# Splitting V's low product into its own matmul, a fourth side bank, and a new order of the query and key transposes in a causal attention kernel

## The reference, cut to what matters

```python
y = x * rsqrt(mean(x * x) + RMS_EPS) * rms_w
y = einsum('bsm,cm->bsc', y, w_in)             # q: 32 heads, k and v: 8 heads, each 64 wide
q, k = rope(q), rope(k)
qk = einsum('bghsd,bgxpd->bghsp', q, k) * 64 ** -0.5
attn = softmax(where(causal, qk, -inf))
o = einsum('bghsp,bgxpd->bghsd', attn, v)      # 4 query heads of a group share k and v
y = einsum('bsc,mc->bsm', o, w_out)            # then x + y, and the feed-forward layer
```

## Time and profile before

| | value |
|---|---|
| median of three runs | 2312.43 us |
| the profiled execution | 2314.37 us, its span 2312.5 us |
| busy share PE, DVE, POOL, ACT | 89%, 68%, 59%, 44% |
| matmuls and weight loads | 17919 and 17919 |
| mean granted TensorE clock | 0.965 of 2.4 GHz |

### The profile page before, as it was taken

The page is one execution under the profiler, slowest core; times in us unless marked ns, Lnnn a source line. Parts: engine busy times, 40 slices in busy tenths (PEclk is TensorE's granted clock), DMA queues, the critical chain, the costliest instruction groups (busy, mean ns, idle before and its releaser), DMA issues. The chain is left out here.

```text
span 2312.5 us, 53405 instructions
## 1 busy us (share of the span) xinstructions
PE 2048.1 (89%) x17919; PEld 1242.3 (54%) x17919; DVE 1572.3 (68%) x2975; ACT 1020.7 (44%) x2216; POOL 1363.8 (59%) x1468
## 2 busy tenths in 40 slices
PE   2489988997998898899889889988989888999998
PEld 1255655565565556556556655655655444444443
DVE  8368867966986796688679668868966666222211
ACT  3245545554555555456555545555554331211210
POOL 5357777785777778577777757777770333212311
PEclk7789999999999999999999999999999999999999
DMA  5421121122112212211221221122116451000000
GB/s 167 133 42 34 34 51 47 31 50 48 34 34 52 49 30 49 48 34 34 52 53 30 46 47 34 34 52 56 31 39 212 159 163 41 1 18 14 5 18 19
DMA packets 228784, 122.74 MB, mean 53 GB/s; under 512 B 187168, under 2 KB 208416, under 8 KB 226976
## 3 DMA queue, kind: packets, MB, share of 16 engines
q1 hardware_dynamic: 228512, 119.26, 20.5%
HBM read 50.53 MB, written 25.17 MB: 33 GB/s over the span
## 5 line engine op out<-in xcount | busy, mean ns | idle before, releaser
L776 POOL TENSOR_TENSOR pl<-p 128x512 f16<-128x512 f32 (+3 forms) x801 | 766.2, 970 | 271.1 <-ACT p L621 269.7
L706 DVE TENSOR_REDUCE mpart<-a_ps 128x1 f32<-128x512 f32 (+3 forms) x1288 | 734.3, 599 | 244.1 <-PE a_ps L538 164.1
L621 ACT ACTIVATE p<-a_ps 128x512 f32<-128x512 f32 (+3 forms) x1283 | 663.9, 532 | 457.0 <-PE a_ps L553 255.3
L568 PE MATMUL a_ps<-v,p 128*128 128x129 f16 x4352 | 555.6, 222 | 28.8 <-DVE pl L698 15.6
L535 PE MATMUL a_ps<-k_hl,q_hh 128*128 128x512 f16 (+3 forms) x1288 | 448.6, 354 | 86.9 <-DVE v L728 51.5
L570 PE MATMUL a_ps<-v,pl 128*128 128x65 f16 x4352 | 519.2, 194 | 0.0
L552 PE MATMUL a_ps<-q_hh,k_hl 128*128 128x512 f16 (+3 forms) x1283 | 453.0, 353 | 55.7 <-DMA q_lm<-qk_lo 55.7
L568 PEld LDWEIGHTS a_ps<-v,p 128*128 128x128 bf16 x4352 | 405.5, 98 | 149.5 <-DVE pl L698 38.8
L553 PE MATMUL a_ps<-q_lm,k_h 128*128 128x512 f16 (+3 forms) x1283 | 451.4, 352 | 0.0
L570 PEld LDWEIGHTS a_ps<-v,pl 128*128 128x128 f16 x4352 | 396.1, 99 | 94.5 <-issue 5.0
L698 DVE TENSOR_TENSOR pl<-p 128x512 f16<-128x512 f32 (+2 forms) x482 | 421.8, 878 | 13.3 <-ACT p L621 13.3
(11 more groups left out here) (99 smaller groups left out, 2762.5 us busy)
## 6 DMA issues: line engine op xcount, KB each, us to landing
attn_scratch<-onorm SPq DMA_DIRECT2D x32, 512.0 KB, 3.0
p_att<-attn_scratch SPq DMA_DIRECT2D x64, 256.0 KB, 3.4
raw<-ffn_t SPq DMA_DIRECT2D x12, 1024.0 KB, 6.9
wraw<-w_in_t SPq DMA_DIRECT2D x9, 768.0 KB, 5.2
resid_scratch<-xin SPq DMA_DIRECT2D x4, 1024.0 KB, 4.3
raw<-w_out_t SPq DMA_DIRECT2D x1, 4096.0 KB, 15.2
x<-resid_scratch SPq DMA_DIRECT2D x4, 1024.0 KB, 6.8
out<-x SPq DMA_DIRECT2D x16, 256.0 KB, 2.0
```

What stands on the lines that cost most here:

```text
L568: nc.tensor.matmul(o, p_high[:, i % RING, t * P:(t + 1) * P], v[:, par, j, 0:VU], start=(j == 0 and t % 2 == 0), stop=False, skip_group_ch ...
L621: nc.scalar.activation(p32[:, i % RING, r * P:CHUNK], sbank(i)[:, r * P:CHUNK], ACT.Exp, scale=SCALE).then_inc(exp_done, 1)
L706: nc.vector.reduce_max(mpart[:, u % 2, t, kk:kk + 1], side_bank(part, ("piece", ahead, u, i))[:, 0:width], AX.X)\
L776: nc.gpsimd.tensor_tensor(pl[:, i % RING, cols], p32[:, i % RING, cols], p_high[:, i % RING, cols], ALU.subtract).then_inc(low_pool, 1)
```

## The change

A value row of V becomes [V high, 1, spare, V low]: the low part starts at column 66 (`VL`). P high now meets [V high, 1] in a matmul of 65 columns, P high again meets V low in one of 64 that adds into the same 64 output columns, and P low meets [V high, 1] as before. Each query tile's output is 65 wide, four fit one bank (260 numbers), and the bank that is freed goes to the side work, which now has four (`SIDE`). ScalarE copies 260 instead of 516 numbers per partition, and GpSimd's `osum` goes. In units where a step has sometimes two pieces they come earlier by up to a slot (`i * n // m == j`), and where a piece comes every few steps it comes at the start of that stretch.

In `TRANSFERS`, `hh` gets a due step six steps ahead of the unit two before its own, `k` moves from 1.5 to 4 steps behind the last low part, and `lm` is due 2.5 slots after the unit's last piece. The opening issues keys after the first `hh`, and the low parts of units 0 and 1 ahead of later ones.

```diff
-VW = DH + 1 + DH + 1
-VU = 2 * DH + 1
+VU = DH + 1
+VL = VU + 1
+VW = VL + DH
...
+SIDE = 4
...
-            pieces = [(ahead, w, i) for i in range(j * m // n, (j + 1) * m // n)]
+            pieces = [(ahead, w, i) for i in range(m) if i * n // m == j]
...
-    timed = [(FIRST_STEP[2] + 2, ("store", 3, -1))]
-    timed += [(FIRST_STEP[HG * (c + 1)] + OUT_LAG + 4, ("store", c, 0)) for c in range(NCH - 1)]
+    timed = [(FIRST_STEP[4] - 2, ("store", 3, -1))]
+    timed += [(FIRST_STEP[HG * (c + 1) + 1] + 4, ("store", c, 0)) for c in range(NCH - 1)]
     for (ahead, c), n in last_proj.items():
         for h in range(HG):
             before = UNITS * ahead + HG * (c - 2) + h
             free = FIRST_STEP[before + 1] + 1
-            timed.append((max(n + QK_LOW_LAG + 1, free), ("hh", c, h, ahead)))
-        timed.append((n + QK_LOW_LAG + 1.5, ("k", c, 0, ahead)))
-    for u in range(UNITS):
-        ahead = int(u == 0)
-        timed.append((FIRST_STEP[(u - 1) % UNITS] + 1.5, ("lm", *divmod(u, HG), ahead)))
+            wanted = UNITS * ahead + HG * c + h - 2
+            wanted = STEPS * (wanted // UNITS) + FIRST_STEP[wanted % UNITS]
+            timed.append((max(n + QK_LOW_LAG + 2, free, wanted - 6), ("hh", c, h, ahead)))
+        timed.append((n + QK_LOW_LAG + 4, ("k", c, 0, ahead)))
+    for n, (_, _, pieces) in enumerate(SLOTS):
+        for ahead, u, i in pieces:
+            if i == KEY_TILES[u] - 1:
+                timed.append((n + 2.5, ("lm", *divmod(u, HG), ahead)))
...
-        side_bank = lambda part, item: ps[:, 3 + side_of(part).index(item) % 3, :]
-        obank = ps[:, 6:8, :]
-        o_read = obank[:, :, 0:2 * VW].rearrange("p a (t w) -> p a t w", w=VW)[:, :, :, 0:VU]
+        side_bank = lambda part, item: ps[:, SBANKS + side_of(part).index(item) % SIDE, :]
+        obank = ps[:, SBANKS + SIDE, 0:TPC * VU]
...
+            query_high(0, 0, 0, 0)
+            keys(0, 0, 0, 0)
+            query_high(0, 0, 1, 0)
+            query_low(0, 0, 0, 0)
+            for h in range(2, HG):
+                query_high(0, 0, h, 0)
+            query_low(0, 0, 1, 0)
+            keys(0, 1, 0, 0)
             for h in range(HG):
-                query_high(0, 0, h, 0)
-            keys(0, 0, 0, 0)
-            query_low(0, 0, 0, 0)
-            for h in range(HG - 1):
-                query_high(0, 1, h, 0)
-            keys(0, 1, 0, 0)
+                if ("hh", 1, h, 1) in TRANSFERS:
+                    query_high(0, 1, h, 0)
...
-                    if r >= 3:
-                        side_read(*side_of(part)[r - 3])
+                    if r >= SIDE:
+                        side_read(*side_of(part)[r - SIDE])
...
-                        o = obank[:, t // 2, (t % 2) * VW:(t % 2) * VW + VU]
-                        nc.tensor.matmul(o, p_high[:, i % RING, t * P:(t + 1) * P], v[:, par, j, 0:VU],
-                                         start=(j == 0 and t % 2 == 0), stop=False, skip_group_check=True)
-                        last = nc.tensor.matmul(o[:, 0:DH + 1], pl[:, i % RING, t * P:(t + 1) * P], v[:, par, j, 0:DH + 1],
+                        o = obank[:, t * VU:(t + 1) * VU]
+                        weights = p_high[:, i % RING, t * P:(t + 1) * P]
+                        nc.tensor.matmul(o, weights, v[:, par, j, 0:VU], start=(j == 0 and t == 0), stop=False,
+                                         skip_group_check=True)
+                        nc.tensor.matmul(o[:, 0:DH], weights, v[:, par, j, VL:VW], start=False, stop=False,
+                                         skip_group_check=True)
+                        last = nc.tensor.matmul(o, pl[:, i % RING, t * P:(t + 1) * P], v[:, par, j, 0:VU],
                                                 start=False, stop=(j == TPC * c + t), skip_group_check=True)
...
-                    nc.scalar.activation(osb[:, u % 2].rearrange("p (a t) w -> p a t w", a=2), o_read,
-                                         ACT.Copy).then_inc(o_out, 1)
+                    nc.scalar.activation(osb[:, u % 2].rearrange("p t w -> p (t w)"), obank, ACT.Copy).then_inc(o_out, 1)
...
-                    nc.gpsimd.tensor_tensor(osum[:, u % 2], osb[:, u % 2, :, 0:DH], osb[:, u % 2, :, DH + 1:VU],
-                                            ALU.add).then_inc(o_sum, 1)
-                    pool.wait_ge(o_sum, g * UNITS + u + 1)
...
-                    nc.gpsimd.tensor_tensor(onorm[:, c % 2, :, h, :], osum[:, u % 2],
+                    nc.gpsimd.tensor_tensor(onorm[:, c % 2, :, h, :], osb[:, u % 2, :, 0:DH],
```

## The result

The changed kernel takes 2226.53 us, the median of four runs (2224.68 to 2228.65), against 2313.05 us before (median of four, one more than ahead of the prediction): ratio 0.9624, 95% interval 0.9613 to 0.9636. Forecast were 2215 us, within 2178 to 2268. Some 86.5 us went, 97.5 had been expected. The profiled execution took 2228.65 us.

What follows compares the result with a forecast made beforehand. No engine is full throughout attention: TensorE waits for q's low parts and side banks, and VectorE is as full in one stretch. Gains of 120.5 less 11 + 12 give 97.5 us off 2314.4: 2217, median 2215 us, range 2178 to 2268.

Steps and rivals of the forecast that it cites:

- deduction of 12: Where VectorE is full, its low parts of P come late and TensorE's waits for them grow: 12 us back, bounds 0 to 30.
- The added matmul: A third matmul and weight load for each of 4352 query tiles costs 2.5 ns each, 11 us, bounds 0 to 185.
- the slower rival: Weight loads don't follow every 30 ns: 42.5 ns more per query tile, 185 us, giving 2389 us; chance 4%.
- The low parts' order: Issuing `lm` earlier on SP removes TensorE's waits for q's low parts: 42 us, plus 6.5 in the first group.
- The clock: Without the idle time before step 32, TensorE's clock doesn't fall: 1.65 us per group, 13 us, bounds 0 to 16.
- The fourth bank: Another side bank removes 42 of 59 us of TensorE's waits for projections' read-out, none where VectorE is full; bounds 8 to 59.
- VectorE would turn the bank's gain into waits for `pl`: Rival: VectorE takes over, bank waits are renamed rather than removed, the bank gives 8 us, total 2245 us; chance 22%.
- The unit's end: ScalarE's shorter copy saves 0.21 us at 40 of 128 unit ends, 8 us; removing `osum` from GpSimd gives 5 us.
- The opening: Before attention, chunk 0's keys go ahead of three `hh` transfers: 4 us gained, bounds 2 and 5.
- The shared port: With 128 fewer GpSimd operations VectorE might gain some 10 us of its time, little on the path; nothing in the sum.
- The signs: Expected: tiles about 88 ns, low-part waits under 12 us, bank waits about 15; wrong if a tile takes over 110 ns.
- the prediction's two cases: Steps without a piece: microcode decode at about 62 ns per matmul costs 8 us in all; hardware decode, floor 25 ns, nothing.

Runs made afterwards that it cites:

- three_banks: The changed kernel with three side banks instead of four, the eighth bank left empty: 2271.39 us, ratio 0.9816.
- old_sp_order: The changed kernel with SP's old list of transfers and old opening; moved pieces, four banks and split stay: 2283.71 us, ratio 0.9867.
- split_only: The kernel before with only the matmul of 129 columns cut into one of 65 and one of 64: 2332.78 us, ratio 1.0069.
- four_short: The changed kernel with V's low product in two matmuls of 32 columns, four matmuls per query tile: 2302.54 us, ratio 0.9948.
- osum_kept: The changed kernel with an addition of osum's size kept on GpSimd at each unit's end: 2233.72 us, ratio 0.9654.
- mixed_width: The changed kernel with three of four query tiles keeping one matmul of 129 columns, only the fourth split: 2239.43 us, ratio 0.9672.

## Why the prediction was right, point by point

- **The sum and its parts.** The runs give two ways from before to the changed kernel. Order alone -40; then split, narrow copy, no osum, still three banks: 0.9828 to 0.9816, -3 (the single prices +16, -10 and -7 give -1); then the fourth bank -44: -87. The other way: everything but the order -31, the order -56. For the second way the forecast had -32 (the bank 42, copy 8, osum 5, less 11 and 12) and -65.5. So its terms were right in kind, and the one that was mis-sized is the order's: 65.5, measured 56.
- **What was luck.** The single prices, the order 56, bank 44, copy 10, osum 7, less 16 for the split, add up to 101 us, and the change gave 86.5; 14.5 are counted twice. The forecast's deduction of 12 has nearly this size, but it stood for longer waits on VectorE's low part, and those didn't grow.
- **Where the time went.** Distances from one step's scores to the next, summed over the eight groups of the profiled execution, in us:

| steps | before | changed | three_banks | old_sp_order |
|---|---|---|---|---|
| 0 to 15 | 225.4 | 213.0 | 219.1 | 216.7 |
| 16 to 27 | 115.1 | 107.2 | 112.5 | 107.2 |
| 28 to 35 | 117.4 | 72.4 | 74.2 | 118.7 |
| 36 to 56 | 239.3 | 237.4 | 247.2 | 237.4 |
| 57 to 95 | 382.6 | 366.3 | 380.4 | 366.3 |
| 96 to 159 | 540.4 | 541.7 | 541.7 | 541.7 |

- **The added matmul.** Predicted 11, measured 16 (12 to 19). Weight loads do follow each other every 30 ns, so the slower rival fell. But the interval behind the 64-column matmul is 32 ns (33 in split_only), not 29, and the tile takes 92 ns and not 88. A limit on short matmuls is close, though far below the rival's 42.5 ns: four_short meets one at 25 to 29 ns.
- **The low parts' order.** Predicted 42 + 6.5 + 13 + 4 = 65.5; measured 56 with four banks, 40 with three. At step 32 the mechanism was right: 1.08 us of wait for the keys in the fourth group, 1.25 in the mean, where 0.8 was forecast. Where the term was wrong is the count: it took all 16 waits, 45.9 us, as removed but for the keys. Only eight of them, 37.0 us, stood at step 32. The others, 8.6 us in seven groups and a 0.4 in the first, stood at step 4 or 8 of a group, and such waits are still there, 10.8 us without the first group. I had the wait at step 8 for the first group alone, but the second TensorE row shows it in the fourth too:

```profile
112.79 0.61 PE L558 MATMUL a_ps<-q_hh,k_hl 128*128 128x512 f16 x1 [5.86 <-DMA q_lm<-qk_lo]
...
687.73 0.39 PE L558 MATMUL a_ps<-q_hh,k_hl 128*128 128x512 f16 x1 [1.26 <-DMA q_lm<-qk_lo]
```

  What is late there is mostly unit 2's maxima, at step 8 in every group. In the fourth VectorE has them at 685.19, SP issues `lm` at 685.26, and TensorE goes on at 687.73. In the first group the wait at step 4 (9.76 us) fell to 1.53 and one of 5.86 came at step 8, where 3 were forecast.
- **The clock.** It stays at its full level from step 28 to 39 in all eight groups, as forecast. But the loss before, 1.65 us, was read in the fourth group, one of two with the shorter low stretch. The third, steps 28 to 39, before (20.6 us, granted clock 0.83) and now (15.5 us, 1.00):

```profile
559.60:580.20 20.60, 16.05 (x148) 10.20 (x145) 12.82 (x26) 7.42 (x16) 11.56 (x13) 0.83 0.24 46
528.00:543.50 15.50, 13.77 (x189) 9.21 (x186) 12.95 (x27) 7.01 (x16) 9.42 (x11) 1.00 0.37 75
```

  Six groups are like it (0.83 to 0.84), two have 0.91 to 0.92. Steps 28 to 35 gave 45 us in all; the waits that went there, less the new one for the keys, are some 27 of these by the waits' rows. That leaves 18 us, an estimate, for the clock and all else there, where 13 were forecast. No run here takes the clock apart from the wait.
- **The fourth bank.** 42 predicted, 44 measured. Two of its reasons failed. That VectorE would turn the bank's gain into waits for `pl` was wrong, at 15.1 us against 15.6 before. And that cover doesn't help where VectorE is full was wrong too: of the 37 us between the changed kernel and three_banks in the table 14 are in steps 57 to 95, where VectorE is busy for 95%, and 23 in steps 0 to 47. So the right size came with a wrong picture of where it lies.
- **The unit's end.** 13 predicted, 17 measured (10 and 7). The row for L568's wait for the copy, 4.7 us of idle time, understates it, since idle time counts from the shown end of the matmul before, 0.16 us after the next could have started.
- **The opening.** 4 us predicted: from TensorE's first matmul to the first group 101.2 - 68.0 = 33.2 us, where it was 104.6 - 67.1 = 37.5: 4.3 us.
- **The shared port.** Osum's removal was to give VectorE a little. Its low part of 512 columns takes 965 ns in the changed kernel, 944 in osum_kept and 959 before, so 128 fewer GpSimd operations don't shorten it. What does set its length is how much of a GpSimd operation is left when it begins. In the changed kernel 85 of these 353 begin with none under way and take 681 ns; 64 begin with 0.4 to 0.6 us left and take 1067; 40 with 0.8 to 1.0 us left and take 1472. They end some 0.55 us behind GpSimd's operation, in the kernel before too. The rule of the Trainium skill (SBUF — State Buffer, section "SBUF: two separate sides") names a lock between the two engines, on which the one that comes second waits for the other. These lengths agree with it, but for the first 0.13 us of overlap, which costs nothing.
- **The signs.** Beside the above, GpSimd's busy time fell by 108 us (some 100 forecast), the waits for q's low parts to 18.8 and not under 12, and no sign of being wrong was met.

## What to carry to other kernels

Before splitting a matmul to save PSUM, compare the time of the parts' columns with the smallest distance between starts in a trace: cutting 129 columns into 65 and 64 cost 5 ns here, and cutting the 64 into two of 32 another 21. In a queue with a fixed order, sort by when the consumer needs a transfer, not by when its input may be ready; then ask which transfer is late next. When a wait is removed, look for others of its kind at other steps before all of them are counted as gone. Fixes that act on the same waits don't add up, so price a fix once alone and once on top of the others, and when a wait for one engine's result remains, try giving just that step to another engine.

## What the runs showed of the hardware that was not expected

- In four_short a matmul with its weight load starts 25 to 29 ns after the one before even when that has 32 columns (13 ns of columns at 2.4 GHz). The Trainium skill (TensorE: Matmul & The Clock Gate, section "Wait — 56ns, not 53.3ns?") gives a floor of about 25 ns between starts. The 25.2 ns behind the second 32-column matmul agree; the average over a tile's four was 28. Its 62 ns per matmul for a sequencer that decodes in microcode don't show here: a step's twelve matmuls run some 31 ns apart, so of the prediction's two cases the second holds.
- Behind a 64-column matmul whose successor loads other weights, the interval is 32.4 ns on average in the changed kernel, 3 ns more than behind one of 65 columns. In mixed_width, where V's low part starts at column 65 and not 66, it is 32.9, so the start isn't the reason; the cause is open.
- A VectorE operation with both inputs in SBUF took 681 ns beside an idle GpSimd and up to 1584 ns beside a busy one (the same shape, the changed kernel).
